# A two-layer graph network on one core: the rows that TensorE gathers itself, from one chunk of 128 edges at a time to four chunks in one 512-column product

## The reference

```
h = x                                   # (3125, 128)
for _ in range(2):                      # passes 0 and 1
    m_ij = relu(concat(h[src], h[dst], edge_attr) @ We1 + be1) @ We2 + be2
    h = h + segment_sum(m_ij, dst)
x = layernorm(x + h + bias)
norm = dinv[src] * edge_weight * dinv[dst]              # pass 2: graph convolution
out = segment_sum((x @ W.T)[src] * norm, dst) + bias1
x = layernorm(x + relu(out) + x)
```

## Time and profile before

| | us |
|---|---|
| median of 3 timed runs | 2697.55 |
| fastest and slowest of them | 2687.21, 2702.28 |
| span of the profiled execution | 3568.7 |
| PE busy in it | 2679.8 (75%) |
| POOL busy in it | 1843.2 (52%) |
| DVE busy in it | 1482.6 (42%) |
| ACT busy in it | 685.7 (19%) |

### The profile page before, as it was taken

The page is one execution under the profiler, slowest core; times in us unless marked ns, Lnnn a source line. Parts: engine busy times, 40 slices in busy tenths (PEclk is TensorE's granted clock), DMA queues, the critical chain, the costliest instruction groups (busy, mean ns, idle before and its releaser), DMA issues.

```text
span 3568.7 us, 72128 instructions
## 1 busy us (share of the span) xinstructions
PE 2679.8 (75%) x24750; PEld 2452.1 (69%) x24750; DVE 1482.6 (42%) x3796; ACT 685.7 (19%) x1685; POOL 1843.2 (52%) x1781
## 2 busy tenths in 40 slices
PE   3788877787777777977777878777878767776775
PEld 2687766777677766766676767677767666666765
DVE  3443333433443433443333333333333655554564
ACT  2010000000000000110000100000000355555553
POOL 3455545454655454266565655556656454444442
PEclk7777778778878777677888787788787877877777
DMA  5222222222222222322222222222222211111111
GB/s 123 65 77 73 67 67 69 68 70 69 72 70 75 65 70 63 90 75 77 77 71 75 75 75 75 69 72 77 75 75 75 59 36 30 33 31 31 31 30 36
DMA packets 186116, 233.28 MB, mean 65 GB/s; under 512 B 77720, under 2 KB 137231, under 8 KB 185876
## 3 DMA queue, kind: packets, MB, share of 16 engines
q0 software_dynamic: 56512, 115.85, 12.0%
q1 hardware_dynamic: 122324, 112.13, 11.6%
q10 hardware_dynamic: 7168, 4.09, 0.4%
HBM read 221.77 MB, written 10.12 MB: 65 GB/s over the span
## 4 chain that ended last, share of the span: by engine, by line
PE 72%; issue 22%; another core or an unknown queue 2%; DVE 2%; DMA 2%; ACT 0%; DVEq 0%; SPq 0%; ACTq 0%
PE ps L580 30%; PE ps L590 14%; PE ps L576 14%; PE ps L677 6%; PE ps L667 5%; PE ps L587 1%; DMA gat<-dst_row 1%; DMA cbase_dram<-cint 1%; PE ps L753 1%; PE ps L749 0%; PE ps L690 0%; PE ps L608 0%; DVE node_b L1079 0%; DVE stats L1388 0%
## 5 line engine op out<-in xcount | busy, mean ns | idle before, releaser
L515 POOL DMA_INDIRECT gat<-p_dram,idx x1438 | 1504.4, 1046 | 1245.5 <-DVE msg L1183 768.0
L580 PE MATMUL ps<-x,node_a 128*128 128x128 bf16 x4900 | 608.8, 253 | 187.2 <-issue 185.7
L855 ACT ACTIVATE msg<-msg 128x512 f32<-128x512 f32 x404 | 253.6, 630 | 2411.3 <-DVE msg L1183 2127.7
L580 PEld LDWEIGHTS ps<-x,node_a 128*128 128x128 bf16 x4900 | 472.4, 116 | 232.6 <-issue 229.1
L576 PE MATMUL ps<-rhs,lhs 96*128 96x128 f32 x3232 | 532.5, 320 | 123.8 <-issue 105.8
L580 PE MATMUL ps<-adj,node_a 128*128 128x128 bf16 x2450 | 554.2, 253 | 93.2 <-issue 92.6
L1183 DVE TENSOR_TENSOR msg<-ps,gat 128x512 f32<-128x512 f32 x404 | 275.6, 688 | 826.2 <-remote 408.9
L576 PEld LDWEIGHTS ps<-rhs,lhs 96*128 96x128 f32 x3232 | 475.6, 227 | 144.7 <-issue 129.2
L580 PE MATMUL ps<-x,adj 128*128 128x128 bf16 x4000 | 476.5, 252 | 118.9 <-issue 118.6
L515 POOL DMA_INDIRECT gat<-z_dram,idx x328 | 326.0, 994 | 391.9 <-PE ps L590 192.5
L580 PE MATMUL ps<-adj 128*128 128x128 bf16 x2000 | 444.9, 252 | 53.9 <-issue 53.8
(11 more groups left out here) (151 smaller groups left out, 2517.2 us busy)
## 6 DMA issues: line engine op xcount, KB each, us to landing
dbc<-dst_row SPq DMA_DIRECT2D x202, 256.0 KB
lhs<-eaT SPq DMA_DIRECT2D x202, 128.0 KB
gat<-p_dram,idx POOLq DMA_INDIRECT x1438
sbc<-src_row SPq DMA_DIRECT2D x202, 64.0 KB
rhs<-q_dram SPq DMA_DIRECT2D x202, 32.0 KB
gat<-z_dram,idx POOLq DMA_INDIRECT x328
idx<-src_g SPq DMA_DIRECT2D x243, 4.0 KB
p_dram<-node_a ACTq DMA_DIRECT2D x12, 256.0 KB, 3.3
```

What stands on the lines that cost most here:

```text
L515: return pool.indirect_dma_start(out=out_, out_offset=None, in_=table, in_offset=bass.IndirectOffsetOnAxis(ap=index, axis=0))
L580: last = nc.tensor.matmul(acc, shot[s][:, t, :], p_part[k][:, t, :], start=False, stop=(t == HI - 1 and k == 2))
L855: nc.scalar.activation(m, m, ACT.Relu).then_inc(relu_done, 1)
```

## The change

A batch is four groups. TensorE still gathers the eighth chunk of a group, but for the four groups of a batch at once, and with the operands exchanged: a piece of P (one block of 128 nodes) is stationary and 512 one-hot columns (four chunks of 128 edges) move. The result is the gathered rows lying on their side, in a PSUM bank of its own (`ps_own`). ACT copies it to SBUF (`own_rows`), and for each group one product with an identity turns 128 of its columns and adds them to the group's PSUM.

- There are 24 batches in a pass, for groups 3 to 98: 96 groups (89 before) in which POOL fetches 7 chunks. Groups 0, 1, 2 and 99 fetch 8, and the last one fetches 7, since its eighth chunk holds padding alone. `gathered` says so. The stretches of ten groups are gone; the loop runs over batches.
- The 25 blocks of a batch are split over the four steps before it as 6, 6, 6 and 7 blocks (`PARTS4`): in each step DVE compares n blocks with 512 sources (`own_hots`), and PE makes 3n products of 512 columns (`own_part`) ahead of `products` and `sums`. `shot` has two buffers.
- `sbc` and `sbc16` hold the sources of four groups; SP loads them once a batch (`source_ids`), in pass 0 after ACT's third split of the weights, since `sbc` lies in that memory.
- DVE adds three chunks instead of four in the second half; ACT takes the relu of the eighth chunk straight from PSUM (one more instruction). The clearing of the eighth slot is gone.
- The splitting of P into pieces moves behind the first one-hots on DVE, and behind the splitting of the weights (pass 0) or a square root (pass 1) on ACT.

```diff
-STRETCH = 10
+BATCHES = (NG - 5) // 4
+OWN_AT = CH - 1
+PARTS4 = [(0, 6), (6, 6), (12, 6), (18, 7)]
...
+        def is_own(g):
+            return type(g) is not int or 3 <= g < NG - 2
+        def gathered(g):
+            return CH - 1 if is_own(g) or g == NG - 1 else CH
...
-            stretch(0)
-            with eng.Fori(1, STRETCHES) as i:
-                stretch(i)
-            step(NG - 1, 0, PAIRS + 1, False, WHOLE[0], False, False)
+            step(0, 0, 1, 1, 0)
+            step(1, 1, 1, 2, 0)
+            step(2, 0, 2, 3, 0)
+            with eng.Fori(1, BATCHES) as q:
+                step(q * 4 - 1, 1, q * 2, 0, q)
+                step(q * 4, 0, q * 2 + 1, 1, q)
+                step(q * 4 + 1, 1, q * 2 + 1, 2, q)
+                step(q * 4 + 2, 0, q * 2 + 2, 3, q)
+            for g in range(4 * BATCHES - 1, NG):
+                step(g, g % 2, g // 2 + 1, 0, None)
...
+                        if p == 0:
+                            sp.wait_ge(w_kept, 3)
+                            row = src_row[3 * GE:7 * GE].rearrange("(a j e) -> a j e", a=1, e=GE)
+                            sp.dma_start(sbc, row[:, :, OWN_AT * P:].to_broadcast([P, 4, P])).then_inc(sbc_in, 16)
...
-                    if own:
-                        for t in range(HI):
-                            for k in range(3):
-                                last = nc.tensor.matmul(acc, shot[s][:, t, :], p_part[k][:, t, :], start=False,
-                                                        stop=(t == HI - 1 and k == 2))
...
+                    def own_part(j, q):
+                        done = batch(p, q) * 4 + j
+                        pe.wait_ge(shot_made, done + 1)
+                        if j == 0:
+                            if not (p == 0 and type(q) is int and q == 0):
+                                pe.wait_ge(own_copied, batch(p, q))
...
+                        t0, n = PARTS4[j]
+                        for t in range(t0, t0 + n):
+                            for k in range(3):
+                                mm = nc.tensor.matmul(ps_own, p_part[k][:, t, :],
+                                                      shot[j % 2][:, t - t0, :, :].rearrange("p j e -> p (j e)"),
+                                                      start=(t == 0 and k == 0), stop=(t == HI - 1 and k == 2))
+                        mm.then_inc(own_mm, 1)
...
+                            last = pre_products(s, h, own=is_own(g))
+                            if h == 1 and is_own(g):
+                                pe.wait_ge(own_copied, batch(p, q))
+                                last = nc.tensor.matmul(ps_pre(s, 1)[:, (OWN_AT % HALF) * P:], own_rows[:, j, :],
+                                                        ident[:, :], start=False, stop=True)
...
-                    def step(g, s, k, first, whole, own, own_next):
-                        if type(g) is not int or g < NG - 1:
-                            products(g + 1, 1 - s, k + s, own_next)
+                    def step(g, s, k, j, q):
+                        if q is not None:
+                            own_part(j, q)
+                        if type(g) is not int:
+                            products(g + 1, 1 - s, k + s, (j + 1) % 4, q + 1 if j == 3 else q)
...
+                            if j == 3 and q is not None:
+                                act.wait_ge(own_mm, batch(p, q) * 4 + 4)
+                                nc.scalar.copy(own_rows[:, :, :], ps_own.rearrange("p (j e) -> p j e", e=P)
+                                               ).then_inc(own_copied, 1)
...
+                            if added < CH:
+                                nc.scalar.activation(msg[s][:, added, :], ps_pre(s, 1)[:, (added % HALF) * P:], ACT.Relu)
...
-                one_hots(0, 0, 1, False)
+                one_hots(0, 0, 1)
                 scatter_hots(0, 0)
+                table_parts()
                 groups(eng, vector_step)
...
-                        V.tensor_scalar(sbc16[:, :], sbc[s][:, :], float(MID), None, ALU.subtract).then_inc(sbc_cut, 1)
...
-                            V.tensor_tensor(shot[s], numbers, sbc16[:, :].unsqueeze(1).to_broadcast([P, HI, P]),
-                                            ALU.is_equal).then_inc(shot_made, 1)
...
+                    def own_hots(j, q):
+                        done = batch(p, q) * 4 + j
+                        if j == 0:
+                            dve.wait_ge(sbc_in, batch(p, q) * 16 + 16)
...
+                            V.tensor_scalar(sbc16[:, :, :], sbc, float(MID), None, ALU.subtract).then_inc(sbc_cut, 1)
...
+                        if not (p == 0 and type(q) is int and q == 0 and j < 2):
+                            dve.wait_ge(own_mm, done - 1)
+                        t0, n = PARTS4[j]
+                        V.tensor_tensor(shot[j % 2][:, 0:n, :, :],
+                                        numbers[:, t0:t0 + n, :].unsqueeze(2).to_broadcast([P, n, 4, P]),
+                                        sbc16[:, :, :].unsqueeze(1).to_broadcast([P, n, 4, P]), ALU.is_equal
+                                        ).then_inc(shot_made, 1)
```

More of the change, by code:

```diff
@@ L244, in build @@
         w_kept = sem("w_kept")
-        sbc_in = [sem(f"sbc_in{s}") for s in range(2)]
+        sbc_in = sem("sbc_in")
         sbc_cut = sem("sbc_cut")
         shot_made = sem("shot_made")
+        own_mm = sem("own_mm")
+        own_copied = sem("own_copied")
         part_cut = sem("part_cut")
@@ L313, in nth @@
             return p * NG + g
-        def rows_of(s, h, use, whole):
-            return 16 * HALF * use if h == 0 else 16 * (HALF - 1) * use + 16 * whole
-        def rows_of3(s, h, i, at, back=0):
-            uses = 2 * (PAIRS + (1 if s == 0 else 0))
-            r = P_TURN if at is None else TURN[:at].count("P")
-            return i * (16 * HALF * P_TURN // 2) + (rows_of(s, h, uses, 2 * WHOLE[s]) + 16 * HALF * (r // 2 + 1 - back))
-        def groups(eng, step):
-            def pair(i, j, own, own_next):
-                g, k = i * STRETCH + j * 2, i * (STRETCH // 2) + j + 1
-                first = type(g) is int and g == 0
-                step(g, 0, k, first, i + 1, own, not first)
-                step(g + 1, 1, k, first, 1, not first, own_next)
-            def stretch(i):
-                pair(i, 0, False, True)
-                with eng.Fori(1, STRETCH // 2 - 1) as j:
-                    pair(i, j, True, True)
-                pair(i, STRETCH // 2 - 1, True, False)
-            stretch(0)
-            with eng.Fori(1, STRETCHES) as i:
-                stretch(i)
-            step(NG - 1, 0, PAIRS + 1, False, WHOLE[0], False, False)
+        def is_own(g):
+            return type(g) is not int or 3 <= g < NG - 2
@@ new lines, in gathered, with rows_of, rows_of3 @@
+        def gathered(g):
+            return CH - 1 if is_own(g) or g == NG - 1 else CH
+        USES = [PAIRS + 1, PAIRS]
+        TAILS = [3 * USES[0] + 2, 3 * USES[1] + 2]
+        def rows_of(p, s, h, g, k):
+            if h == 0:
+                return 16 * HALF * used(p, s, k)
+            wide = 1 if type(g) is int and g in (0, 1) else 2 if s == 0 or (type(g) is int and g == NG - 2) else 1
+            return k * 48 + 16 * (p * TAILS[s] + wide)
+        def rows_of3(h, i, at, back=0):
+            n = i * (P_TURN // 2) + TURN[:at].count("P") // 2 + 1 - back
+            return n * (16 * HALF) + rows_before3(TURN[:at].count("P") % 2, h)
@@ L343, in used, with batch @@
+        def batch(p, q):
+            return p * BATCHES + q
         def used(p, s, k):
@@ L440, in load @@
                         if old:
-                            sp.wait_ge(sbc_cut, nth(p, g) - 1)
-                        row = src_row[bass.ds(g * GE + GE - P, P)].rearrange("(a n) -> a n", a=1)
-                        sp.dma_start(sbc[s][:, :], row.to_broadcast([P, P])).then_inc(sbc_in[s], 16)
-                        if old:
                             sp.wait_ge(pre_mm, 2 * (nth(p, g) - 1))
                         sp.dma_start(lhs[s][W:W + CE, :], eaT[:, bass.ds(g * GE, GE)]).then_inc(ea_in[s], 16)
+                        if j == 0 and q is not None:
+                            source_ids(q)
                         if type(g) is int and g == 0:
@@ L460, in _ @@
                     if p < 2:
+                        if p == 0:
+                            sp.wait_ge(w_kept, 3)
+                            row = src_row[3 * GE:7 * GE].rearrange("(a j e) -> a j e", a=1, e=GE)
+                            sp.dma_start(sbc, row[:, :, OWN_AT * P:].to_broadcast([P, 4, P])).then_inc(sbc_in, 16)
+                        else:
+                            source_ids(0)
                         groups(sp, load)
@@ L523, in _, with gather @@
                 with pool.If(fast == 1):
-                    def gather(g, s, k, first, whole, own, own_next):
+                    def gather(g, s, k, j, q):
                         pool.wait_ge(idx_in[s], 16 * used(p, s, k))
```

(4 more changed lines are left out.)

162 lines of the change are left out of this document (85 added, 77 removed).

## The result

| | before | after |
|---|---|---|
| median of 4 timed runs, us | 2699.91 | 2770.41 |
| lowest and highest | 2687.21, 2712.51 | 2764.02, 2781.37 |
| ratio after / before | | 1.0272 (95%: 1.0229 to 1.0316) |
| span of the profiled execution, us | 3568.7 | 2762.2 |

What follows compares the result with a forecast made beforehand. The prediction took GpSimd's (POOL's) row fetches as the bound of the timed execution: 2697.55 us, less 21.5 for fewer rows, plus 10 for later starts, gave 2686 us, range 2610 to 2770.

Steps and rivals of the forecast that it cites:

- A: Case that POOL (GpSimd) keeps the pace in the loops: 2665 to 2705 us, likeliest 2686; chance 0.46.
- the profiled span of 3260 us: Whole profiled execution: if TensorE's pauses go with instructions, 38% of 785 us vanish, leaving about 3260 us.
- rival C: TensorE's instruction count causes the 149 us above POOL's floor; 38% fewer instructions give about 2630 us; chance 0.20.
- The 149 us above POOL's floor: Whole kernel: the timed median lies 149 us above POOL's floor of 2549 us, in waits that couldn't be placed.
- I take zero and keep 8 a pass: VectorE holding POOL's rows: busy time changes by about a tenth, moving the hold 8 us either way; booked as zero.
- 16 rows fewer, 21.5 us: POOL's row fetches: 711 a pass instead of 719, at 1.346 us each, 21.5 us gained in all.
- The starts, 10 us: Start of each pass: POOL restarts later behind VectorE's additions, 6 us in pass 0 and 4 in pass 1.
- The 215 ns for a product of 512 columns: TensorE's gather: 215 ns a product, 387.5 us a pass, 14.6 us more than before.
- C': TensorE's 512-column product takes much less than four of 128 (131 ns by the skill's page): 2530 to 2600 us; chance 0.05.
- D: VectorE's comparison loses its pace; at half pace up to 290 us more, 2975 us; chance 0.04.
- The turn: TensorE's product with the identity, one per own group: 0.23 us each, 22 us a pass, off the path.
- Rival B: TensorE becomes the bound in pass 0's loop when the granted clock is below 0.91: 2757 us; chance 0.25.

Runs made afterwards that it cites:

- b_merge: The kernel before with VectorE's 16-bit conversion moved ahead of the destinations' one-hot, so one-hot and comparison run without a gap: 2759.9 us, 1.0249 of before.
- b_nocmp: The kernel before with VectorE's comparison cut from 25 blocks to 4 after the first of each pass: 2509.6 us, 0.9347 of before.
- b_psum: The kernel before with the comparison's sources kept in a PSUM bank instead of SBUF, full result computed: 2506.2 us, 0.9353 of before.
- b_wide: The kernel before with a group's 75 gather products of 128 columns replaced by 19 of 512, results left out of the sums: 2693.5 us, 1.0041 of before.
- a_break: The changed kernel with VectorE waiting for its own one-hot before the comparison, in the three steps without a conversion: 2668.9 us, 0.9918 of before.
- a_nope: The changed kernel with 3 products of 512 columns in each gather part instead of 18 or 21: 2770.3 us, 1.0324 of before.

## Why the prediction was wrong, point by point

- *The bound.* GpSimd was named as the bound of the timed execution, and is; the case called A. That the pauses of the earlier trace rows belong to that one execution and not to the timed ones was right as well. That they go with the number of instructions was wrong, and with it the profiled span of 3260 us and rival C: b_merge, b_nocmp and b_psum have 49,500 instructions on TensorE and its loads as before has, and their profiled spans (2758.0, 2508.8, 2500.1) are those of their timed runs. b_wide, with 29,400, gains nothing.
- *The 149 us above POOL's floor.* This is the first step that failed. The floor used's 1.046 us a row, a mean from an execution in which GpSimd waited 768.0 us for `msg`; a comparison that runs while GpSimd waits holds no row. With no pauses it is 1.121 us (b_wide), and (1.121 - 1.046) x 1438 = 108 of the 149 us are rows held. Most of the waits that I couldn't place were this.
- *"I take zero and keep 8 a pass" for VectorE.* The step that gave the wrong sign. I summed VectorE's busy time, which did fall, and let the hold scale with it. The hold depends on what stands next to what. I booked the conversion, 23 us a pass before, as work saved; it was the gap between two instructions that each hold GpSimd. The earlier trace rows had the held row, but I did not ask where it would have been able to start. Measured: 81 us in two passes where zero was booked. 45 of them lie in the step itself, and there a_break's wait brings 273 us back to 198; 28 lie behind the one-hots of the sums, with the cause open, and 8 belong to the starts.
- *16 rows fewer, 21.5 us.* Their 20 us are there. But seven of the eight a pass came with a comparison each, whose hold I had left out; at before's 1.31 us it is as long as the row spared (1.24 us).
- *The starts, 10 us.* Half of what it was. In pass 0 the additions come later by about as much as was said (7 us; 6 were booked), since the splits now stand ahead of them; GpSimd restarts at 87.86, where the earlier trace rows had 81.01:

```profile
87.86 1.25 POOL L540 DMA_INDIRECT gat<-p_dram,idx  x1 [11.55 <-DVE msg L1247]
```

  With a second wait of 3.20 us at 111.29, that is 12 us more than b_wide waits. In pass 1 (4 us booked) GpSimd has no wait at the start; one row is held there for 8.5 us instead, behind the one-hots and all 14 instructions of the splits, which end at 1180.47:

```profile
1171.87 9.42 POOL L540 DMA_INDIRECT gat<-p_dram,idx  x1 [0.30 <-issue]
...
1171.50 0.74 DVE L1187 TENSOR_SCALAR lhs<-dbc,base_p 64x1024 f32<-64x1024 int32 x1 [0.95 <-DMA dbc<-dst_row]
1172.16 0.68 DVE L1085 TENSOR_TENSOR hot<-iota_row,drel 128x512 f32<-128x512 f32 x1
1172.77 3.89 DVE L1205 TENSOR_TENSOR node_b<-node_a,x 128x512 f32<-128x512 f32 x7
1176.58 3.89 DVE L1210 TENSOR_TENSOR adj<-node_b,x 128x512 bf16<-128x512 f32 x7
```

- *TensorE.* The 215 ns for a product of 512 columns hold; the starts are 0.215 us apart in the first three rows here, at full clock:

```profile
621.00 0.38 PE L660 MATMUL ps<-node_a,x 128*128 128x512 bf16 x1
621.22 0.38 PE L660 MATMUL ps<-node_a,adj 128*128 128x512 bf16 x1
621.43 0.59 PE L660 MATMUL ps<-node_a,x 128*128 128x512 bf16 x2
```

  The 131 ns that the prediction quotes from the Trainium skill are not seen, and C' falls. The comparison's 1.75 and 2.04 us hold as well (mean 1.814), and D falls. The turn took 0.3 us (0.23 expected), in TensorE's spare time.
- *Rival B* gave 2757 us and the right side, and is wrong in its cause: a_nope takes five sixths of the gather from TensorE and the time stays.

## What to carry to other kernels

Where GpSimd issues indirect DMAs all the time, count VectorE's instructions with two operands in SBUF (and one-operand ones such as the one-hot here) as time that GpSimd's rows can lose, and look at which of them touch: one-hot and comparison back to back held the rows for 1.7 us a step, with a gap of 0.04 us between them for 1.1. A small instruction between two large ones can be worth more as a gap than it costs; removing it is not a saving until the trace says so. Before a busy engine is given less work, take one operand of the offender out of SBUF: here that was worth 6.5%, with a comparison nearly twice as long.

## What the runs showed of the hardware

- In the rows shown, a fetch held by VectorE ends 0.80 to 0.83 us behind the end of the instruction that held it, whatever that instruction's length (0.74 to 3.34 us).
- A wait of VectorE for its own instruction leaves about 0.04 us, and GpSimd gets its row through in it (86 of 86 in a_break).
- TensorE's single products about 0.7 us apart, 450.6 us of "issue" before the gather's products in one profiled execution of before, are missing in three other profiles with the same number of instructions, where the gather's products have no such wait. What caused them stays open.
